# Writing out the unit loops of VectorE, ScalarE, GpSimd and the transfer queue in a quantized attention and FFN layer

## The reference

```python
# attention: 32 query heads, 8 key/value heads of 128
q = h @ dequant(q_codes, q_scales)      # (code - 8) * scale per group of 128 rows
k, v = h @ dequant(k_...), h @ dequant(v_...)
q, k = rope(q), rope(k)                 # pairs turned by position
attn = softmax(q @ k.T * 128**-0.5 + causal mask)
out = (attn @ v) @ dequant(o_codes, o_scales)
# ffn: 512 -> 1376 -> 512
h = silu((x @ gate_w.T) * gate_s) * ((x @ up_w.T) * up_s)
out = (h @ down_w.T) * down_s
# layer
x = x + layernorm(attention(layernorm(x)))
x = x + layernorm(ffn(layernorm(x)))
```

## Time and profile before

| what | value |
|---|---|
| median of the runs | 1514.34 us |
| the profiled execution | 1515.25 us, span 1513.4 us, mean granted clock 0.983 |
| busy: PE, VectorE, ScalarE, GpSimd | 1423.1, 1094.0, 992.9, 1000.6 us |
| chain that ended last | PE 69%, DMA 7%, issue 7%, SyncE's queue 5%, GpSimd 5%, VectorE 3% |
| instructions recorded | 38106 |
| instruction packets | queue 8: 89, 1.46 MB; queue 14: 68, 0.56 MB |

### The profile page before, as it was taken

How to read it: one execution, slowest core, us unless ns; L and a number is a source line. 1 busy time by engine, 2 the same in 40 slices (tenths; PEclk the granted TensorE clock), 3 DMA queues, 4 the chain that set the end, 5 groups by cost and what they waited for, 6 DMA issues and landing times.

```text
span 1513.4 us, 38106 instructions
## 1 busy us (share of the span) xinstructions
PE 1423.1 (94%) x11104; PEld 853.0 (56%) x11104; DVE 1094.0 (72%) x2469; ACT 992.9 (66%) x2582; POOL 1000.6 (66%) x704
## 2 busy tenths in 40 slices
PE   5789699999999999999999999999999967999998
PEld 2455466656665666566666666665666643454543
DVE  7757477777777777777777777777777786776744
ACT  2566677777777777787777777777777763232321
POOL 2467688878878887888788878887888851110100
PEclk9999899999999999999999999999999988999999
DMA  8379899998888888888899898888988864011000
GB/s 272 67 150 179 167 168 183 166 162 168 168 169 162 170 166 167 166 172 168 165 165 161 168 162 164 166 168 162 171 171 166 170 122 80 15 49 42 15 29 28
DMA packets 522589, 216.77 MB, mean 143 GB/s; under 512 B 478944, under 2 KB 480704, under 8 KB 522432
## 3 DMA queue, kind: packets, MB, share of 16 engines
q1 hardware_dynamic: 519968, 210.53, 70.5%
q0 software_dynamic: 2464, 4.23, 1.6%
HBM read 55.32 MB, written 4.19 MB: 39 GB/s over the span
## 4 chain that ended last, share of the span: by engine, by line
PE 69%; DMA 7%; issue 7%; SPq 5%; POOL 5%; DVE 3%; ACT 2%; DVEq 1%; POOLq 0%; ACTq 0%
PE ps_p L813 7%; PE ps_p L815 7%; PE ps_p L814 7%; PE ps_p L837 6%; PE ps_p L838 5%; DMA ot<-o_parts 4%; PE ps_s L1046 4%; PE ps_s L1047 4%; PE ps_s L852 3%; PE ps_s L850 3%; PE ps_s L851 3%; PE ps_o L868 3%; PE ps_o L867 3%; PE ps_o L866 3%; PE ps_p L1060 2%
## 5 line engine op out<-in xcount | busy, mean ns | idle before, releaser
L511 POOL TENSOR_TENSOR p_lo<-prob,p_hi 128x1280 f16<-128x1280 f32 x128 | 335.6, 2622 | 178.7 <-ACT p_hi L659 158.3
L1137 DVE SCALAR_TENSOR_TENSOR y<-ps_p,wo_scale,y 128x512 f32<-128x512 f32 x512 | 380.9, 745 | 79.0 <-PE ps_p L838 77.4
L650 ACT ACTIVATE prob<-prob,exp_bias 128x512 f32<-128x512 f32 (+3 forms) x512 | 285.5, 558 | 12.5
L1150 DVE CUSTOM_DVE_ANT_0 prob<-ps_s,mask 128x512 f32<-128x512 f32 (+3 forms) x512 | 237.4, 483 | 68.0 <-PE ps_s L852 62.8
L813 PE MATMUL ps_p<-x_hi,w_hi 128*128 128x512 f16 x640 | 244.6, 382 | 2.8 <-DVE x_lo L1105 1.4
L814 PE MATMUL ps_p<-x_lo,w_hi 128*128 128x512 f16 x640 | 244.4, 382 | 0.0
L815 PE MATMUL ps_p<-x_hi,w_lo 128*128 128x512 f16 x640 | 244.2, 382 | 0.0
L837 PE MATMUL ps_p<-ot,wo 128*128 128x512 f16 x512 | 198.3, 387 | 48.6 <-DMA ot<-o_parts 42.0
L868 PE MATMUL ps_o<-v_hi,ffn_w 128*128 128x128 f16 x1280 | 221.0, 219 | 0.0
L866 PE MATMUL ps_o<-v_hi,ffn_w 128*128 128x128 f16 x1280 | 221.0, 219 | 0.0
L867 PE MATMUL ps_o<-v_lo,ffn_w 128*128 128x128 f16 x1280 | 221.0, 219 | 0.0
(11 more groups left out here) (102 smaller groups left out, 2941.5 us busy)
## 6 DMA issues: line engine op xcount, KB each, us to landing
swap<-other SPq DMA_DIRECT2D x320, 128.0 KB, 2.6
w_code<-w_codes SPq DMA_DIRECT2D x36, 384.0 KB, 3.3
w_scale<-w_scales SPq DMA_DIRECT2D x36, 384.0 KB, 4.4
o_code<-o_codes SPq DMA_DIRECT2D x35, 256.0 KB, 3.0
swap<-x SPq DMA_DIRECT2D x16, 256.0 KB, 2.8
out<-z SPq DMA_DIRECT2D x16, 256.0 KB, 2.0
ffn_w<-x SPq DMA_DIRECT2D x3, 1024.0 KB, 9.9
ffn_w<-p_hi SPq DMA_TRANSPOSE x128, 3.5
```

What stands on the lines that cost most here:

```text
L511: pool.tensor_tensor(p_lo[:, :], prob[:, hp, :], p_hi[:, :], ALU.subtract).then_inc(p_lod, 1)
L650: act.activation(prob[:, hp, a:a + w], prob[:, hp, a:a + w], ACT.Exp, bias=exp_bias[:, hp, i:i + 1], scale=-1.0, accum_out=exp_sum[:, hp, ...
L1137: dve.scalar_tensor_tensor(tile, ps_p[:, bank, :], scale, tile, ALU.mult, ALU.add).then_inc(o_add, 1)
L1150: dve.tensor_tensor_reduce(prob[:, hp, P_AT[i]:P_AT[i] + w], ps_s[:, bank, col:col + w], mask[:, S - w:], -SCORE_SCALE, NO_MINIMUM, ALU.ad ...
```

## The change

The three two-unit loops and the four-unit loop become Python loops, so units 2 to 29 of SyncE, GpSimd and ScalarE, and 2 to 30 of VectorE, are written out one after the other with constants for all targets and addresses. In `load_w` the test `isinstance(n, int)` goes, since n is now always a number. What each unit does is not changed.

```diff
--- before.py
+++ after.py
@@ -344,7 +344,7 @@
             def load_w(n, buf):
 
 
-                if isinstance(n, int) and n < KT + 2:
+                if n < KT + 2:
                     after(sp, w_prod, n - 1)
                 else:
                     sp.wait_ge(w_lod, n - 1)
@@ -454,9 +454,8 @@
 
             unit(0, 0, first=True)
             unit(1, 1)
-            with sp.Fori(1, UNITS // 2 - 1) as p:
-                for r in range(2):
-                    unit(2 * p + r, r)
+            for U in range(2, UNITS - 2):
+                unit(U, U % 2)
             unit(UNITS - 2, 0, more=False)
             unit(UNITS - 1, 1, slots=LAST, more=False, last=True)
             turn_o(UNITS * HG - 2, 0)
@@ -583,9 +582,8 @@
             pool.wait_ge(xt_lo, NT)
             pool.dma_start(gate_w[:, :, :], gate_t.rearrange("(k p) f -> p k f", p=P)).then_inc(ffn_in, 16)
             pool.dma_start(up_w[:, :, :], up_t.rearrange("(k p) f -> p k f", p=P)).then_inc(ffn_in, 16)
-            with pool.Fori(1, UNITS // 2 - 1) as p:
-                for r in range(2):
-                    unit(2 * p + r, r, FULL)
+            for U in range(2, UNITS - 2):
+                unit(U, U % 2, FULL)
             unit(UNITS - 2, 0, FULL)
             unit(UNITS - 1, 1, LAST, last=True)
             o_low(UNITS * HG - 2)
@@ -744,9 +742,8 @@
 
             unit(0, 0, FULL, first=True)
             unit(1, 1, FULL)
-            with act.Fori(1, UNITS // 2 - 1) as p:
-                for r in range(2):
-                    unit(2 * p + r, r, FULL)
+            for U in range(2, UNITS - 2):
+                unit(U, U % 2, FULL)
             ffn_scales()
             unit(UNITS - 2, 0, FULL)
             unit(UNITS - 1, 1, LAST, last=True)
@@ -1285,10 +1282,8 @@
 
             unit(0, 0, FULL, first=True)
             unit(1, 1, FULL)
-            with dve.Fori(0, UNITS // NB - 1) as p:
-                for i in range(NB):
-                    unit(NB * p + 2 + i, (2 + i) % NB, FULL)
-            unit(UNITS - 2, NB - 2, FULL)
+            for U in range(2, UNITS - 1):
+                unit(U, U % NB, FULL)
             unit(UNITS - 1, NB - 1, LAST, last=True)
 
             def hidden_low(c, f):
```

## The result

The changed kernel takes 1505.32 us in the median of four runs (1503.36 to 1506.95), the kernel before 1514.78 beside it. The ratio is 0.9935, 95% interval [0.9917, 0.9952]: 0.65% faster, which is 9.8 us, between 7.3 and 12.6 (the two medians lie 9.5 us apart). One more run of before, of 1547.8 us at a mean granted clock of 0.932 instead of 0.98, was in a slower state of the chip and stays out of all ratios.

What follows compares the result with a forecast made beforehand. TensorE, busy 94%, was taken as the bound, its loop-stretch waits nearly all for `ot`, at most 18.0 us to win. Terms -13.6 - 0.5 + 1.5 = -12.6 us from 1514.34 gave 1502 us, range 1496 to 1510.

Steps and rivals of the forecast that it cites:

- The signs: Traces to confirm it: no VectorE "issue" idle, no unit over 37 us, about 7 `ot` waits, some 20 more packets.
- VectorE's six jumps: VectorE's loop in the attention units: its jumps and 12.6 us of idle time go, winning 13.6 us on PE.
- the floor of 35.75: Undisturbed time in us of one looped unit, between two `v_hi`; 28 units at it take 1001.0 us.
- The other three loops: Loops of ScalarE, GpSimd and SyncE: jumps of 54 to 68 ns go, PE does not wait there; 0 taken.
- Register instructions: Register work on the sequencers goes, mostly hidden already; 0.5 us won, ends 0 and 4.4.
- What is issued stays: Same DMAs, sizes, order and semaphores; no wait added, nothing moved past a queue.
- Packets: Instruction packets beside `ot` transfers: 21 more of 8 KB, PE's own hitting twelve units; 1.5 us lost, ends 0 and 9.0.
- The event at 140 to 163 us: Gate and up weight loads fill the DMA engines, PE stands some 10 us; change 0, 4 us either side.
- fetching eats a good part: Rival: instruction packets delay `ot`, costing 5 to 9 us of the gain; 1506 to 1510 us, chance 0.16.
- No gain: Rival: another chain, GpSimd's row of work, is as late and takes over; 1512 to 1516 us, chance 0.07.
- straight-line code stalls: Rival: written-out code stalls at block boundaries, slower, 1585 us if every packet stalls, 1511 to 1521 if few; chance 0.05.
- The rest goes too: Rival: shorter sequencer work gives `ot` room, the other units' 4.4 us shrink as well; 1496 to 1499 us, chance 0.10.

Runs made afterwards that it cites:

- e1: Kernel before with only VectorE's loop written out, the loops of ScalarE, GpSimd and SyncE kept: 1505.48 us, ratio 0.9931.
- e2: Kernel before with ScalarE, GpSimd and SyncE written out, VectorE still looped: 1516.34 us, ratio 1.0007.
- e12: Kernel before with VectorE's loop in two-unit passes as e3, but 36 instructions fewer, 297 records a pass: 1506.18 us, ratio 0.993.
- e4: Changed kernel with a four-unit loop on ScalarE, 566 records a pass: 1505.81 us, ratio 0.9931.
- e8: Changed kernel measured again, nothing altered: 1506.77 us, ratio 0.9946.
- e9: Changed kernel with ScalarE's old two-unit loop, padded by six semaphore increments a head, 334 records a pass: 1506.43 us in one run.
- e6: Changed kernel with GpSimd computing the low part of `o_parts` before the two rope remainders in head h = 2: 1498.78 us, ratio 0.9884.
- e10: e6 with the gate and up weights in eight loads, spread over units 2 to 9, instead of two: 1489.56 us, ratio 0.9818.
- e5: Kernel before with VectorE's loop in two passes of twelve units, one jump, its last five looped units written out: 1510.24 us, ratio 0.9964.
- e13: Changed kernel with ScalarE's old two-unit loop, padded by ten semaphore increments a head, 366 records a pass: 1515.92 us in one run.
- e3: Kernel before with VectorE's loop in two-unit passes, 13 jumps over 333 records, batch entry in a register: 1534.38 us, ratio 1.0129.
- e7: Kernel before with GpSimd's order of e6 alone, all loops kept: 1509.15 us, ratio 0.9951.

## Why the prediction was right

Forecast 1502 us, range 1496 to 1510, measured 1505.3. The mechanism was right, the gain 9.8 us instead of 12.6. The signs came out: no unit over 37 us, no idle time of VectorE before `prob` and `low` but two pieces of 0.24 us, seven waits of PE, 15 more packets on queue 14. One wait of `exp_bias` was 2.04 us, a hair over the 2 that were named, and the 28 units took 1009.6 us, where 1006 had been forecast.

1. *VectorE's six jumps, 13.6 us.* Shown by e1 (all of the gain), e2 (none of it) and e12 (jumps that find their code resident cost nothing). The size was too high. The twelve units at and behind the jumps were 13.6 us over the floor of 35.75; 2.9 of these are left in the changed kernel, mostly where PE meets its own code packets, so the jumps were worth 10.7. The prediction took VectorE's idle time as the length of the stall; the stall is 3.0 to 4.6 us long, and the idle time is what VectorE's queued work did not cover.
2. *The other three loops, 0.* Shown by e2. Their passes stay resident: behind each of their jumps back the sequencer goes on after 0.2 to 0.3 us.
3. *Register instructions, 0.5.* No effect that a run could tell: e2 loses those of three engines and is at 1.0007; e12 keeps them on all four engines and is as fast as the changed kernel.
4. *What is issued stays.* Nothing in the traces speaks against it.
5. *Packets, 1.5 lost.* This is the term that was mis-sized. The 28 units cost 1009.55 - 1001.0 = 8.6 us over the floor; I had forecast 18.0 - 12.6 = 5.4. The twelve freed units kept 2.9 us where 1.5 was booked: the full rate of the other units (0.28 x 12 = 3.4) would have been nearer than half of it. The other sixteen cost 5.7 us where the sum had 4.4 - 0.5 = 3.9; in the traces of e1, e4, e8, e9 and e12 they cost 4.5 to 6.3. Seven waits of PE make up 6.0 of the 8.6 us, and at each a packet of PE's code lies beside the transfer of `ot` (4.62 us in the row above against 3.05 alone). All seven are for the transfer whose `o_parts` GpSimd makes last in the head h = 2, with 0.7 us of slack. e6 shows that it is this slack: with 1.6 us more of it the seven waits and 4.3 us are gone. The 8 KB packets, which I feared, came out at 15 more (83 against 68 on the page), and transfers with only such a packet beside them landed after 3.2 us in the mean, against 3.1.
6. *The event at 140 to 163 us, 0.* It stayed. e10 shows that the two loads issued there cause it, and what it costs.

Of the rivals, "fetching eats a good part" holds a piece of the truth, with PE's packets in the place of those of the other engines. "No gain" and "straight-line code stalls" are out: some 65 packets of 8 KB are used up in the written-out stretch, and VectorE, ScalarE and GpSimd have no piece of idle time "issue" over 0.24 us there. "The rest goes too" did not happen by itself; e6 makes it happen.

What stays open: the last 1 to 3 us of e5, and why 334 records fit on ScalarE and 333 on VectorE do not; whether it matters where a pass begins within the 8 KB packets was not tried. Why the runs of one kernel spread over 8 us was not tried either; both kernels do it, and in two traces of the changed one the 28 units differ by 0.8 us only.

## What to carry to other kernels

Before writing out a loop, look behind its jumps for idle time that no semaphore explains, and count the instructions of one pass in the trace: with up to 297 on VectorE and 334 on ScalarE the jump was free, with 333 and 366 the sequencer waited 3 to 5 us for the first instruction of its target. Read that wait in the sequencer's own records on the line of the loop, since queued work hides part of it from the engine's idle time. Shortening the pass (e12) is worth as much as writing it out, and a stall is paid only where its engine's next product has less slack than the idle time is long (e4, e13). What then remains is found at the place with the least slack: moving one operation of GpSimd ahead of two others and cutting two large loads in eight brought another 1.2% (0.9818 against 0.9935), where the whole rewrite had brought 0.65%.

## What the runs showed of the hardware

- A jump back finds its code resident up to a size of the pass: 297 records fit and 333 did not on VectorE (e12, e3), 334 fit and 366 did not on ScalarE (e9, e13). The number of instructions alone does not set the border. On ScalarE 32 instructions more turned 41 packets of code into 100 from 300 to 1180 us, and 0 us of idle time into 56.0.
- When the target is not resident, its first instruction comes 2.9 to 5.5 us behind the branch, on VectorE and on ScalarE (before, e2 to e5, e7, e13); when it is, 0.2 to 0.3 us. The wait did not grow with the pass: 3.9 us in the mean with 333 records (e3) as with 653 (before), 4.4 with 1949 (e5, one jump).
- A pass that stays resident needs almost no code packets: 2 on queue 14 in 880 us with all four engines looped (e12). The Trainium skill (Advanced Engine Details and Errata, "ISA Cache") gives 32 KB for an engine other than TensorE, in two lines of 16 KB with 256 instructions each, 512 together. The packets of queue 14 are 8 KB here, and passes of 333 and 366 records did not stay, so here the measurement decides.
- With a 16 KB packet of PE's own code beside it, and no other, a transpose of `ot` took 4.4 us in the median of 22 (3.1 to 4.9); with no packet 3.1.
- In the written-out stretch of the changed kernel (190 to 1190 us) VectorE, ScalarE and GpSimd show no piece of idle time "issue" over 0.24 us, and none at all between 139 and 163 us, while 2.75 MB of weights were being loaded.
